# Attention scores two heads further ahead, with the maxima of all heads placed in sixteen marked rows

## The reference

```python
t = t + attn(ln(t))                       # t: 16 images x 256 tokens x 128
sq = (x @ wq_s) * scale; sk = x @ wk_s    # 8 heads of 16
search_sim  = einsum('bsid,bsjd->bsij', sq, sk)
search_attn = softmax(search_sim, axis=-1)
retrieved   = einsum('bsij,brjd->bsird', search_attn, rv)   # 2 values
...                                       # a gate between the two values, then w_out
t = t + ffn(ln(t))                        # router, top 2 of 8 experts, silu
```

## Time and profile before

| what | value |
|---|---|
| median of 3 executions | 687.31 us (682.93 to 689.00) |
| the profiled execution, and its span | 685.38 us, 683.6 us |
| PE busy | 566.0 us, 83% of the span |
| DVE, ACT, POOL busy | 475.9, 333.1, 262.6 us |
| first shifted scores of image 0 | 191.95 us after the start |
| last shifted scores' exponent | ends at 470.07 us |
| scatter's last transfer issued, experts begin | 494.5 us, about 497 us |

### The profile page before, as it was taken

How to read it: one execution, slowest core, us unless ns; L and a number is a source line. 1 busy time by engine, 2 the same in 40 slices (tenths; PEclk the granted TensorE clock), 3 DMA queues, 4 the chain that set the end, 5 groups by cost and what they waited for, 6 DMA issues and landing times. The chain is left out here.

```text
span 683.6 us, 10705 instructions
## 1 busy us (share of the span) xinstructions
PE 566.0 (83%) x3180; PEld 439.7 (64%) x3180; DVE 475.9 (70%) x1227; ACT 333.1 (49%) x718; POOL 262.6 (38%) x328
## 2 busy tenths in 40 slices
PE   5999999849788988979898887876169999999910
PEld 4888888636565767666666665654058888888810
DVE  6886774855557777777878778785537767767715
ACT  3322302233356465554636355544148888888800
POOL 3245443458000100141413314247603666666660
PEclk9999999959879999999999999998569999999965
DMA  7994145649531405041230505001278777776109
GB/s 262 365 347 145 57 170 185 203 164 372 153 116 39 155 1 155 1 151 36 96 92 31 157 3 184 9 25 48 76 251 293 234 243 230 246 235 221 51 6 363
DMA packets 55224, 105.46 MB, mean 154 GB/s; under 512 B 8744, under 2 KB 21689, under 8 KB 55040
## 3 DMA queue, kind: packets, MB, share of 16 engines
q1 hardware_dynamic: 50176, 96.24, 42.6%
q0 software_dynamic: 4992, 8.54, 3.6%
HBM read 58.15 MB, written 48.42 MB: 156 GB/s over the span
## 5 line engine op out<-in xcount | busy, mean ns | idle before, releaser
L1949 POOL DMA_INDIRECT y_slots<-virt,pad_l x92 | 95.7, 1041 | 72.5 <-DVE virt L2001 49.5
L1280 DVE TENSOR_REDUCE s_max<-bank 128x2 f32<-128x512 f32 x128 | 87.4, 689 | 40.3 <-PE bank L1596 39.8
L1059 ACT ACTIVATE s_expd<-bank 128x512 f32<-128x512 f32 x128 | 76.9, 602 | 53.5 <-PE bank L1617 52.3
L973 POOL DMA_INDIRECT x_slots<-rows,slot_of x64 | 63.1, 986 | 55.9 <-DVE rows L1408 38.3
L937 POOL TENSOR_TENSOR ln_rstd<-ln_var,power 128x4 f32<-128x4 f32 x17 | 17.4, 1026 | 173.4 <-DVE ln_var L1256 173.4
L1989 DVE TENSOR_TENSOR k_stack<-virt,k_stack 128x512 fp32r<-128x512 f32 x92 | 63.4, 689 | 24.9 <-ACT k_stack L1968 24.2
L1632 PE MATMUL bank<-s_expd,rvx 128*64 128x256 f32 x512 | 70.5, 397 | 1.5 <-ACT s_expd L1059 1.0
L61 PE MATMUL bank<-pad_h,u_h 128*128 128x512 f32 x144 | 59.9, 416 | 8.4 <-DVE pad_l L399 8.4
L1617 PE MATMUL bank<-q_stack,k_stack 100*128 100x256 f32 x256 | 61.8, 325 | 5.0 <-DVE q_stack L1298 5.0
L1968 ACT ACTIVATE k_stack<-virt 128x512 fp32r<-128x512 f32 x92 | 58.2, 633 | 10.1 <-PE bank L63 7.2
L1963 ACT ACTIVATE virt<-bank 128x512 f32<-128x512 f32 x92 | 55.0, 597 | 14.3 <-PE bank L63 13.9
(11 more groups left out here) (260 smaller groups left out, 1321.8 us busy)
## 6 DMA issues: line engine op xcount, KB each, us to landing
x_slots<-blank SPq DMA_DIRECT2D x8, 2112.0 KB, 17.3
pad_h<-w_split SPq DMA_DIRECT2D x23, 512.0 KB, 4.4
q_stack<-w_split SPq DMA_DIRECT2D x23, 512.0 KB, 5.7
qk_rows<-qk SPq DMA_DIRECT2D x16, 512.0 KB, 3.0
k_stack<-qk_rows SPq DMA_DIRECT2D x96, 64.0 KB, 2.4
q_stack<-qk_rows SPq DMA_DIRECT2D x48, 128.0 KB, 2.6
pad_l<-x_slots SPq DMA_DIRECT2D x23, 264.0 KB, 5.2
e_raw<-in_w SPq DMA_DIRECT2D x16, 256.0 KB, 3.0
```

The lines of the kernel that those rows point to most:

```text
L973: pool.indirect_dma_start(out=x_slots[:, :], out_offset=bass.IndirectOffsetOnAxis(ap=slot_of[:, ring, k, j:j + 1], axis=0), in_=rows[:, ri ...
L1059: nc.scalar.activation(expd[:, s % 4].rearrange("p a i -> p (a i)"), ps_st[s % 2][:, :], ACT.Exp).then_inc(exp_done, 1)
L1280: nc.vector.tensor_reduce(s_max[:, :, s], ps_s[s % 2][:, :].rearrange("p (a j) -> p a j", a=2), AX.X, ALU.max).then_inc(max_done, 1)
L1949: pool.indirect_dma_start(out=y_slots[:, :], out_offset=bass.IndirectOffsetOnAxis(ap=ids, axis=0), in_=y_rows[:, t % 2, j, :], in_offset=N ...
```

## The change

Five things change together.

1. `scores` run two heads further ahead: step s of image i now carries head s + 2 of image i + 1, and steps 6 and 7 carry heads 0 and 1 of image i + 2 (`ahead_of`). DVE's `row_max_ahead` follows at the same step, with `split_max` right after head 7, at step 5. PE's `turn_max` moves from the end of an image to its step 6, after the retrieve and the scores there.
2. The maxima of all eight heads (high and low: 16 rows) are turned at once into the scores' own bank (`max_bank`), and one ACT copy places them in rows 96 to 111 of `q_stack` for all four pairs (16 x 1024 elements); `place_max` of DVE is gone. `k_stack` marks by ones in rows 96 to 111 which head is meant (`mark_heads`, a POOL copy for each ring, in place of 24 fills), and shifted scores use 112 rows.
3. `head_q` moves from step 0 of the next chunk to the end of the body, behind `head_k` (FIRST still has its own at step 0).
4. On DVE `route` moves one step later, `add_attention` and `norm_stats` one step later, `normalise_t2` of MIDDLE from the first half's end to step 0 of the second half, `place` from step 7 to step 6; four `low` steps of the last images move from before the first maxima into the first body.
5. At the start, scores of image 0 use four banks; the queries of chunk 0 are sent from ACT's queue, the keys from SP's.

```diff
+    LEAD = 2
+    TURN_AT = S - LEAD
+    def ahead_of(image, s):
+        image, s = image + 1 + (s + LEAD) // S, (s + LEAD) % S
+        return (image, s) if image < 2 * NCH else None
+    def score_bank(image, s):
+        return ps_s[(9 * image + s - (1 if s else 2)) % 2]
+    def max_bank(image):
+        return ps_s[9 * image % 2]
...
 # ACT
-        def place_max(g, b, ring, src=ps_x):
-            act.wait_ge(m_turned, 2 * g + b + 1)
-            for p in (2, 3):
-                nc.scalar.activation(q_stack[96:100, ring, p, b * PIX:(b + 1) * PIX],
-                                     src[32 * p:32 * p + 4, 0:PIX], ACT.Copy).then_inc(m_odd, 1)
+        def place_max(image):
+            act.wait_ge(m_turned, image + 1)
+            at = image % 2 * PIX
+            wide = max_bank(image)[0:2 * S, 0:PIX].unsqueeze(1).broadcast_to([2 * S, NP, PIX])
+            nc.scalar.activation(q_stack[MAX_AT:MAX_AT + 2 * S, image // 2 % 2, :, at:at + PIX], wide, ACT.Copy
+                                 ).then_inc(m_placed, 1)
...
+            place_max(2 * g + 1)
             keep_pair(g, 0, NP - 1)
-            place_max(g, 1, ring, max_bank(stage))
...
 # PE
+        def scores_in_turn(image, s):
+            if s == 0:
+                pe.wait_ge(max_done, S * image - 1)
+            elif s == 2:
+                pe.wait_ge(m_placed, image)
+            else:
+                pe.wait_ge(max_done, S * image + max(s - 1, 1))
+            scores(image, s, score_bank(image, s))
+        def scores_ahead(image, s):
+            if at := ahead_of(image, s):
+                scores_in_turn(*at)
+            if s == TURN_AT and image + 1 < 2 * NCH:
+                turn_max(image + 1)
...
                 shifted_scores(g, 1, s, ring)
-                if stage != LAST:
-                    scores(g + 1, 0, s, 1 - ring)
+                if s != TURN_AT:
+                    scores_ahead(2 * g + 1, s)
                 pairs_behind(g, 1, s, ring)
+                if s == TURN_AT:
+                    scores_ahead(2 * g + 1, s)
...
-            if stage != LAST:
+            if ahead:
                 need(pe, spot_read, 4 * (g - 2) + 1)
-                turn_max(g + 1, 0)
-            if ahead:
                 head_k(g + 2)
+                head_q(g + 2)
...
 # DVE, second half
+                row_max_ahead(2 * g + 1, s)
                 if stage == MIDDLE and s == 0:
                     add_conv(g + 2)
+                if stage != FIRST and s == 0:
+                    normalise_t2(g - 1, 1 - ring)
...
 # ACT, start
         keep_tok(0, 0, 0)
+        bounce_first_q()
         keep_tok(0, 1, 0)
+        split_zt(1)
+        stack_first_q()
```

More of the change, by code:

```diff
@@ L740, in token_attention @@
     s_neg = sb("s_neg", [P, 2, S], where=ctx)
-    m_split = sb("m_split", [P, 2, NP, 32], F32R, ctx)
+    m_split = sb("m_split", [P, 2, S, 2], F32R, ctx)
+    head_of = sb("head_of", [2 * S, S], where=ctx)
     expd = sb("s_expd", [P, 4, 2, PIX], where=ctx)
@@ L879, in chunk, with bounce, fill_k @@
     def chunk(tensor, g):
         return tensor[:, bass.ds(g * CH, CH)]
+    def bounce(queue, g, first, signal):
+        queue.dma_start(qk_rows[bass.ds(g, 1), first:first + 2].rearrange("g n c t -> c (g n) t"),
+                        f32(qk[:, first:first + 2, :])).then_inc(signal, 16)
+    def fill_k(queue, g, ring, b):
+        at = slice(b * PIX, (b + 1) * PIX)
+        for slot, n in enumerate((0, 0, 1)):
+            src = qk_rows[bass.ds(g, 1), n, :, at].rearrange("g (p a r) t -> a r (g p) t", p=NP, a=2)
+            for a in range(2):
+                row = 32 * slot + D * a
+                queue.dma_start(f32(k_stack[row:row + D, ring, a:S:2, at]), src[a]).then_inc(stacked[b], 16)
@@ L882, in _, with fill_q @@
+    def fill_q(queue, g, ring, b):
+        at = slice(b * PIX, (b + 1) * PIX)
+        for slot, n in enumerate((2, 3, 2)):
+            src = qk_rows[bass.ds(g, 1), n, :, at].rearrange("g (p r) t -> r (g p) t", p=NP)
+            queue.dma_start(f32(q_stack[32 * slot:32 * slot + 32, ring, :, at]), src
+                            ).then_inc(stacked[b], 16)
     @block.sync
     def _(sp):
-        def stack(g, ring):
[L888 to L906, removed]
@@ L1418, in body @@
                         low_q(g + 1)
+                if stage == FIRST and s in (2, 3, 4, 5):
+                    low(10 + s)
                 if stage != FIRST:
@@ L1700, in body @@
                 shifted_scores(g, 0, s, ring)
-                scores(g, 1, s, ring)
+                if s != TURN_AT:
+                    scores_ahead(2 * g, s)
                 pairs_behind(g, 0, s, ring)
+                if s == TURN_AT:
+                    scores_ahead(2 * g, s)
+                if stage == FIRST and s == 0:
+                    head_q(g + 1)
                 if stage != LAST:
-                    if s == 0:
-                        head_q(g + 1)
                     if s == 3:
@@ L1805, in _ @@
         head_turn_back(1, 2)
-        conv_taps(2, range(4, 8), ps_pv[0])
+        conv_taps(2, range(4, 9), ps_pv[0])
         head_k(1)
         for s in range(S):
-            scores(0, 0, s, 0)
-            if s == 0:
-                conv_taps(2, range(8, 9), ps_pv[0])
-        turn_max(0, 0)
-        pe.wait_ge(ones_made, 3 * S)
+            need(pe, max_done, s - 3)
+            scores(0, s, first_banks[s % 4])
+        scores_in_turn(1, 0)
+        turn_max(0)
+        scores_in_turn(1, 1)
+        pe.wait_ge(ones_made, 2)
         pe.wait_ge(t_ready, 3)
```

200 lines of the change are left out of this document (92 added, 108 removed).

## The result

The changed kernel takes **695.37 us** (median of 4 executions, 694.41 to 697.59) against 686.09 us before, a ratio on record of 1.0126 with a 95% interval of 1.0081 to 1.0172 (the two medians alone give 1.0135; ratios below are those on record too). It is 1.3% slower; the forecast was 684.1, with a range up to 690.5. One execution of `e1_mark_later` took 1119.12 us, slower than all others, and does not enter its ratio. The profiled execution's span is 695.8 us against 683.6; it is the slowest of its four (697.59), while the one before lies near its median (685.38), so that the traces differ by 12.1 us where the medians differ by 9.3.

A forecast was written before the change was run, and what follows sets the result against it. PE's own work fills first halves; in second halves PE and DVE hand work to each other, neither full. Terms -2.5 + 3.3 + 3.6 - 7.6 = -3.2 us, from the 687.31 median, gave 684.1 us; range 677.5 to 690.5.

The forecast's parts named there:

- Start: Kernel start to the first shifted scores: 2.5 us shorter, bounds -3.5 to -1.2.
- the step on POOL: At the start: POOL's two marking copies cost nothing; if longer, chunk 1's norm comes up to 1 us later.
- on two queues the loads land some 0.6 earlier: At the start: keys sent from SP and queries from ACT make the loads land some 0.6 us earlier.
- Second half: Second half of a middle chunk: 17.5 us, 1.5 more than before, with a 1.2 us PE wait; lower bound 16.4.
- The 1.00 us that DVE waited for scores: Second half of a middle chunk: this DVE wait falls away because scores run ahead, against 1.1 us added by normalise_t2.
- the chain that was added up, through the exponent: End of the second half: 13.1 to head 7's exponent, then 2.0, 0.7, 0.9 and 0.8, giving 17.5 us.
- I take one such fall again: Chunks 1 to 5: one fall of TensorE's clock, as before, costing 1.4 us, within a +3.6 us term.
- rival (b): Even boundaries: the clock falls at each, six falls in place of one, 691 to 696 us; chance 0.12.
- First body: Images 0 and 1: image 0 waits at step 6 for chunk 1's stacked rows; +3.3 us, bounds +1 to +4.
- First halves: First half of a middle chunk: 20.8 us, a gain of 1.1 to 1.2, since o_tok comes 1.1 earlier.
- the last images: Images 12 to 15, last two chunks: a shorter boundary chain and earlier work, together -7.6 us, bounds -9.5 to -5.
- the experts behind are untouched: Behind the last images: the experts' part stays as it was, with no term in the sum.

The follow-up runs named there:

- e1_mark_later: Changed kernel with POOL's second marking copy moved behind the normalise of chunk 1's rows; 690.88 us, ratio 1.0055 to the kernel before.
- e2_turn_later: Changed kernel with PE's turn of the maxima in second halves put behind the shifted scores of head 7; ratio 1.0132 to the kernel before.
- e4_norm_back: Changed kernel with normalise_t2 put back at the end of the first half; ratio 1.0181 to the kernel before.
- e7_step7: e2_turn_later with three more order changes at step 7 of second halves, on PE, ACT and DVE; 684.88 us, ratio 0.9930 to the kernel before.
- e3_fill: Changed kernel with unused PE products filling both second-half waits, ahead of the turn and ahead of head_k; ratio 1.0067 to the kernel before.
- e9_mark_fill: Changed kernel with the edits of e1_mark_later and e3_fill together; 685.39 us, ratio 0.9953 to the kernel before.
- e12_best_tail: Changed kernel plus e1_mark_later, e7_step7, chunk 0's queries on SP's queue, and chunk 5 scattered before chunk 6's rows are copied; 674.75 us, ratio 0.9801.
- e5_mark_pieces: Changed kernel with POOL's marking copy cut into eight copies of 16 x 512 at the same place; 694.14 us, one execution.

## Why the prediction was wrong

**Start (-2.5 forecast, +3.0 measured): the step on POOL failed.** It said of the marking copies "I put them at nothing, hidden by its wait for DVE's sums". That asks who waits for POOL; POOL was indeed idle. It does not ask whom POOL holds. DVE stood still beside a copy of 3.59 us, PE waited 3.25 for DVE, and the clock fell behind that wait; `e1_mark_later` gives 5.9 us of it back at the first shifted scores, of which 1 to 2 are this one execution's. Without the copy there, the start is 188.97, near the 189.45 forecast. The Trainium skill, "Advanced Engine Details and Errata", section "Mode Summary", says that VectorE's second SBUF port is shared with GpSimd, so that GpSimd's instructions and VectorE's two-port ones block each other; the trace agrees that they block (4.47 against 1.11), though no row shows which ports `z_tok` uses. The row that could have told stood in the trace of before: 1.77 us for `z_tok` beside the fills, where the same four take 1.1 without company. A smaller term had the wrong sign: "on two queues the loads land some 0.6 earlier". From the split of the queries to the first scores it takes 0.7 longer than on SP's alone (9.46 against 8.76 us). The stretch from the first scores on was right and better than forecast (7.9, forecast 8.6).

**Second half: the number right, by luck, the reason not.** 17.5 us were forecast, 17.75 came; the wait ahead of the turn 1.2 and 1.11; head 7's exponent 13.1 and 12.9. But the wait was not what set the end, nor `normalise_t2` what made it. Taking away the one (`e2_turn_later`) or the other (`e4_norm_back`) leaves the half as long as it was. The 1.00 us that DVE waited for scores was said to fall away "since scores run ahead"; without `normalise_t2` it is there again, 1.07, so that the 1.1 added and the 1.0 taken off are one and the same stretch. And the chain that was added up, through the exponent, was not the last: when the exponent had ended, at 382.2, ACT waited 0.52 for the turned pair, at the end of the chain through DVE's split, the maximum of head 0, the scores of head 1 and the turn. From the exponent's start to the end of `zt_h` it took 2.5 us in place of 2.0; `head_k` and `head_q` took 1.45 in place of 1.7, and hid half of that. Only `e7_step7`, which shortens both chains, shortens the half, by 1.45 us. The sum would have shown it if it had been made for each instruction that stands ahead of `zt` on ACT.

**The clock: "I take one such fall again" failed.** There were three in five chunks, rival (b), which had 0.12. The step that set the mechanism aside ("four of the five chunks had no fall before") took rows of halves without the added wait for evidence on halves with it. The size of a fall, 1.4, was near: 1.6 by `e3_fill`, nearly all of it in the second half itself. Which of PE's waits it takes, and in which chunk, stays open. The rule that the prediction quotes from the Trainium skill's "TensorE: Matmul & The Clock Gate" points the right way: with work that nothing uses in the waits, the clock stays up and the half is as long.

**First body (+3.3 forecast, +5.7 measured).** The mechanism was right: image 0 waits for chunk 1's rows, 1.91 us. The rest is the clock again, at 1.2 GHz for 10.5 us of these two images after against 4.7 in `e9_mark_fill`, where they take 32.3 us, +3.9. (The terms of image 0 add up to 15.1, not 15.3; it took 17.0 after, 15.8 in `e9_mark_fill`.)

**First halves (20.8 forecast, 20.65) and the last images (-7.6 forecast, -6.6)** came as worked out: 16.1, 13.3 and 13.0 us for images 12 to 14 against 15.6, 12.8 and 13.4, ACT's copy 1.01. But "the experts behind are untouched" failed by 1.8 us. The scatter was named as what could prove me wrong, and it did in part: POOL issues from 472.95 on without a pause, the root of image 14's tiles stands behind that, and 1.2 us of the images' gain go back; `e12_best_tail` recovers 1.0. The other 0.6 lie behind the scatter, and are no more than what one execution differs from another there: from the last scatter issued to the end, the sixteen traces take 189.0 to 190.7 us, the one before 189.1, the one after 189.7.

With the copy moved and the waits filled, and nothing else touched, the ratio is 0.9953, which is that of the forecast, 684.1 to 687.31. That the two are equal is luck (the interval is 0.3% to either side, and in the table the middle is 0.8 us below the forecast and what lies behind the last exponent 1.6 above). But it says that the two things left out, a copy that holds another engine and the clock, make up nearly all of the miss, and not the order of the work.

## What to carry to other kernels

An instruction on an idle engine is free only if it also holds nobody: beside each long GpSimd instruction that a change adds, look at what VectorE does in the same microseconds, and at rows of the kernel before where the two already run together. When a wait is added to a stage that repeats, count the falls of TensorE's clock in each repetition as a term of the sum; products that nothing uses, put into the wait, show in one run what the wait costs through the clock alone. A wait that is plain to see need not set the end: before moving it, follow the queue of the engine that makes the next input, instruction by instruction, and look for a second chain that ends in the same microsecond.

## What the hardware showed that I had not expected

A GpSimd copy of 16 x 4096 elements (3.59 us) holds VectorE's `TENSOR_SCALAR` from SBUF to SBUF for all its length, though it touches 16 partitions only; cut in eight of about 0.56 us, it holds them for 1.3 us in all (2.39 against 1.11), since VectorE gets in between two. A subtraction of two SBUF tensors is held as well (1.24 against 0.69), a sum with an operand in PSUM was not (0.68 at 166.71 in `e5_mark_pieces`, 0.67 at 166.69 in the kernel before, with POOL at work beside both). Of two waits of 1.1 and 1.3 us in the same half, 4.5 us apart, filling the first alone brought the time down by as much as filling both, and filling the second alone did not; why the place should matter, no run shows, and the profile with the first filled has two falls all the same.
